# A recommendation tower on one core: six moves issued by the POOL instead of ACT, and two steps of the drain put elsewhere

## What is computed

```python
x = layer_norm(dense_t @ Wd.T, gd, bd)
y = layer_norm(jnp.einsum('bnd,ed->bne', sparse_t, Ws), gs, bs)
y = jnp.einsum('bne,pn->bep', y, Wsi)
y = layer_norm(y, gsi, bsi)
T = jnp.concatenate([x[:, None, :], jnp.swapaxes(y, 1, 2)], axis=1)
Z = jnp.einsum('bnd,bmd->bnm', T, T)
z = layer_norm(Z[:, TRIL_I, TRIL_J] @ Wl.T, gl, bl)      # the first 384 of 512 are kept
h = jnp.concatenate([z, r_dense_t], axis=1)
h = jnp.maximum(h @ W_top1 + b_top1, 0.0)
h = jnp.maximum(h @ W_top2 + b_top2, 0.0)
y = h @ W_top3
```

## Time and profile before

| | us |
|---|---|
| median of 3 timed runs | 590.68 |
| lowest and highest | 590.22, 592.27 |
| the profiled execution | 590.11 |
| its span, first to last instruction | 588.3 |
| PE busy in the span | 523.2 (89%) |
| DVE busy | 431.7 (73%) |
| POOL busy | 394.8 (67%) |
| ACT busy | 339.3 (58%) |

### The profile page before, as it was taken

One profiled execution on the slowest core, in us unless ns is written; L12 is line 12 of the kernel. 1 busy time (PEld: TensorE's weight loads), 2 busy tenths in 40 slices (PEclk: granted clock), 3 DMA queues, 4 the chain that ended last, 5 costly groups with the idle time before them and its releaser, 6 DMA issues.

```text
span 588.3 us, 11685 instructions
## 1 busy us (share of the span) xinstructions
PE 523.2 (89%) x4327; PEld 382.3 (65%) x4327; DVE 431.7 (73%) x806; ACT 339.3 (58%) x731; POOL 394.8 (67%) x420
## 2 busy tenths in 40 slices
PE   0557889597999999997999999998999999989888
PEld 0435656474778667776677767766777767856657
DVE  3579998689677977697877967796787977787210
ACT  1235666466657765575766765675657765766223
POOL 5777777777777777777777777777777777750000
PEclk9997999899899999999999999999999999999999
DMA  6911121212111121212121221212121211110100
GB/s 214 372 47 26 28 54 27 53 28 52 29 42 38 39 62 28 52 30 71 28 46 33 45 56 35 45 31 69 29 52 27 52 31 43 38 34 17 27 0 1
DMA packets 28152, 29.89 MB, mean 51 GB/s; under 512 B 9784, under 2 KB 20544, under 8 KB 27712
## 3 DMA queue, kind: packets, MB, share of 16 engines
q0 software_dynamic: 13312, 13.66, 12.2%
q1 hardware_dynamic: 14456, 15.29, 8.2%
q10 hardware_dynamic: 328, 0.20, 0.1%
HBM read 23.01 MB, written 0.01 MB: 39 GB/s over the span
## 4 chain that ended last, share of the span: by engine, by line
POOL 46%; PE 26%; issue 19%; DMA 4%; DVE 3%; ACT 1%; ACTq 1%; POOLq 0%; SPq 0%
POOL emb L314 46%; PE bank_h L442 5%; PE bank_u L405 4%; DMA emb<-in_tables,ids 3%; PE bank_m L465 3%; PE bank_y L416 3%; PE bank_g L391 2%; PE bank_z L430 2%; PE bank_t L382 2%; PE bank_t L430 1%; PE bank_m L526 1%; DVE part L910 1%; ACTq L774 1%; PE bank_g L490 1%; PE bank_m L533 0%
## 5 line engine op out<-in xcount | busy, mean ns | idle before, releaser
L314 POOL DMA_INDIRECT emb<-in_tables,ids x416 | 394.6, 949 | 130.3 <-issue 123.1
L662 ACT ACTIVATE sq<-tt 128x512 f32<-128x512 f32 x128 | 131.1, 1133 | 4.6 <-DVE tt L963 3.4
L932 DVE TENSOR_TENSOR prod<-bank_g,emb 128x512 f32<-128x512 f32 (+1 forms) x64 | 37.6, 588 | 89.0 <-PE bank_g L391 88.5
L442 PE MATMUL bank_h<-wz,zr 128*128 128x512 f32 x192 | 93.2, 610 | 3.1 <-ACT zt L727 2.1
L405 PE MATMUL bank_u<-mix_w,emb 128*128 128x192 f32 (+4 forms) x512 | 86.0, 314 | 9.7 <-DVE emb L951 9.7
L405 PEld LDWEIGHTS bank_u<-mix_w,emb 128*128 128x128 f32 x512 | 80.3, 200 | 10.9 <-DVE emb L951 10.9
L963 DVE TENSOR_TENSOR tt<-bank_y,biasc 128x512 f32<-128x512 f32 x128 | 81.9, 681 | 2.5 <-PE bank_y L416 2.5
L644 ACT COPY embt<-bank_t 128x512 f32<-128x512 f32 (+1 forms) x64 | 32.5, 507 | 82.4 <-PE bank_t L382 82.2
L980 DVE TENSOR_TENSOR tt<-tt,bank_z 128x1024 f32<-128x1024 f32 x64 | 78.1, 1220 | 2.2
L970 DVE TENSOR_REDUCE ssum<-sq 128x32 f32<-128x1024 f32 x64 | 77.5, 1211 | 1.1 <-ACT sq L662 1.0
L416 PE MATMUL bank_y<-us,proj 64*128 64x512 f32 x256 | 73.0, 647 | 0.7 <-ACT us L654 0.7
(11 more groups left out here) (121 smaller groups left out, 622.5 us busy)
## 6 DMA issues: line engine op xcount, KB each, us to landing
emb<-in_tables,ids POOLq DMA_INDIRECT x416, 2.4
zs<-zbig SPq DMA_DIRECT2D x62, 40.5 KB
zs<-zbig SPq DMA_DIRECT2D x62, 36.0 KB
dense<-in_dense SPq DMA_DIRECT2D x8, 256.0 KB, 5.1
wfull<-in_wfull SPq DMA_DIRECT2D x1, 2048.0 KB, 10.2
wz<-in_wrows SPq DMA_DIRECT2D x1, 1536.0 KB, 13.2
w<-in_w SPq DMA_DIRECT2D x1, 1280.0 KB, 13.9
zs<-zbig SPq DMA_DIRECT2D x62, 16.5 KB
```

The costliest lines, as they stand in the source:

```text
L314: pool.indirect_dma_start(emb[:, e, t, D * a:D * a + D], None, x_in["tables"], bass.IndirectOffsetOnAxis(ap=ids[:, col:col + 1], axis=0),) ...
L442: mm = pe.matmul(bank_h[:, :], zr[:, s, :], wz[:, s, :], start=(s == 0), stop=(s == SLOTS - 1))
L662: A(sq[:, GRP * a:GRP * a + GRP, :].rearrange("p (q w) v -> p q v w", w=WIDE), tt[:, u % 2, q0:q0 + n, C0:ZC, :], ACT.Square).then_inc(sq_ ...
```

## The change

Three things. The six moves of unit 15 that ACT issued (`move_rest`) are gone from ACT; the POOL issues them after its last gather, behind the same three waits, and they count up a semaphore of their own, `zs_rest`, for which `z_rows(15)` waits besides. `gains_z(14)` is due one step sooner, TAIL+5, which puts it behind `relu1(6, 0)` and ahead of `z_rows(15)`. And `open_last` is put from behind `top2(6)` (TAIL+6) to behind `turn_z(15)` and `top3(6)` (TAIL+7), ahead of `last1(0)`.

```diff
 def gains_z_of(s):
     if s > TAIL + 2:
-        return {TAIL + 6: NU - 2, TAIL + 8: NU - 1}.get(s)
+        return {TAIL + 5: NU - 2, TAIL + 8: NU - 1}.get(s)
     return unit(s, GAINZ_AT)
...
+            pool.wait_ge(zc_ok, 4 * NR * NU)
+            pool.wait_ge(sumcol_ok, NU)
+            pool.wait_ge(zr_ok, NU - 1)
+            for j in range(2, 4):
+                for part in range(3):
+                    pool.dma_start(rows_to(j, part), rows_from((NU - 1) % 2, j, part)
+                                  ).then_inc(zs_rest, 16)
...
-                if s == TAIL + 6:
-                    open_last()
                 i = x_of(s, 0)
...
                 j = top3_of(s)
                 if j is not None:
                     top3(j)
+                if s == TAIL + 7:
+                    open_last()
                 a = half_of(s, LAST1_AT)
...
             def z_rows(u):
-                act.wait_ge(zs_in[u % 2], 12 * 16 * (u // 2 + 1))
+                if u < NU - 1:
+                    act.wait_ge(zs_in[u % 2], 12 * 16 * (u // 2 + 1))
+                else:
+                    act.wait_ge(zs_in[u % 2], 12 * 16 * (u // 2) + 6 * 16)
+                    act.wait_ge(zs_rest, 6 * 16)
                 after(act, flat_done, u)
...
-            def move_rest():
-                act.wait_ge(zc_ok, 4 * NR * NU)
-                act.wait_ge(sumcol_ok, NU)
-                act.wait_ge(zr_ok, NU - 1)
-                for j in range(2, 4):
-                    for part in range(3):
-                        act.dma_start(rows_to(j, part), rows_from((NU - 1) % 2, j, part)
-                                      ).then_inc(zs_in[(NU - 1) % 2], 16)
...
-                if pd == (NU - 1, 3):
-                    move_rest()
```

More of the change, by code:

```diff
@@ L268, in dlrm @@
         xcol_ok, z_done, zc_ok, sumcol_ok = sem("xcol_ok"), sem("z_done"), sem("zc_ok"), sem("sumcol_ok")
-        zs_in, zr_ok = [sem("zs_in0"), sem("zs_in1")], sem("zr_ok")
+        zs_in, zs_rest, zr_ok = [sem("zs_in0"), sem("zs_in1")], sem("zs_rest"), sem("zr_ok")
         flat_done, hst_ok, hmv_ok, hstd_ok, hrs_ok, zn_ok = (
```

## The result

The changed kernel took 592.26 us at the median of 22 timed runs (590.27 to 593.93), the kernel before beside it 590.21 (589.73 to 592.59): a ratio of 1.0027, 95% interval 1.0016 to 1.0038. The medians lie 2.05 us apart and the ratio says 0.27%, or 1.6 us: small, but clear of no change, and several times the +0.27 us (0.05%) of the sum. The times of both kernels lie in groups: before, 17 runs from 589.73 to 590.68 and 5 from 592.03 to 592.59; after, 5 from 590.27 to 591.08, 13 from 591.88 to 592.94, and 4 from 593.58 to 593.93. Between the lowest groups there is little, and the changed kernel is seldom in its lowest group. The profiled execution (592.19, span 590.4) is of the middle one.

What follows compares the result with a forecast made beforehand. The prediction took the drain to be bound by a chain of waits between ACT and PE, after a body paced by gathers. Its terms, -1.48 - 0.05 + 1.80 = +0.27 us, on the 590.68 median gave 590.95; range 589.1 to 592.6.

Steps and rivals of the forecast that it cites:

- the sum: In the drain after the body: -1.48 for moves, -0.05 for scaling, +1.80 for open_last, together +0.27 us.
- moves: Six issues leave ACT, so the first rectified pair, relu1(6, 0), starts at 552.76 instead of 554.24: 1.48 us earlier.
- scaling and copy in place of the pair: On ACT before the wide-weights product: scaling and copy take 2.00 us where rectified pair and scaling took 2.05, saving 0.05.
- open_last: Sixteen matmuls moved from PE's idle window before the transposes to its gapless stretch behind the third layer: +1.80 us.
- rival 4: Scaling on ACT not gated, copy comes as the moves land, product starts at 558.62: -1.4 us, 589.3; chance 0.06.
- Rival 1: PE has slack behind the third layer, or open_last held up the transposes, so its cost isn't paid in full: 589.15; chance 0.12.
- The POOL's price: Each of the POOL's six moves costs one gather, 1.25 us start to start; the last lands at 557.74.
- The slack before the copy was due: Moves, due on ACT at about 559.35, have 1.6 us to spare at one gather's price.
- rival 2: POOL issues slowly and delays the product: 0.3% slower at 1.86 us per issue, 595.6 at 2.5; chance 0.18.
- Rival 3: PE's new idle 2.0 us before the transposes brings the lower clock, costing up to 2.5 us: 593.4; chance 0.04.

Runs made afterwards that it cites:

- the own tile: Changed kernel, open_last back behind the second layer, unit 14's scaled rows in a separate tile: 586.76 us, ratio 0.9926; a second version kept ACT's moves, ratio 1.0012.
- open_last back: Changed kernel with open_last returned to behind the second layer (TAIL+6), the POOL's moves and earlier scaling kept: 591.29 us, ratio 0.9985.
- the control: The changed kernel unaltered, measured once more (also called "again") on the chip of three other kernels: 592.64 us, ratio 1.003.
- both gaps filled: Changed kernel with eight calls of matmuls nobody uses, 1.8 us, in each of PE's two idle gaps: 591.06 us, ratio 0.9995.

## Why the prediction was right, and where it wasn't

**The sum.** At the upper level of the clock it is +0.29 to +0.31 us against +0.27, and each term by itself came out: -1.46 for -1.48 (moves), 0.00 for -0.05 (scaling and copy in place of the pair), +1.79 for +1.80 (open_last). What carried it was reading the condition in `gains_z`. By rival 4, the naive reading, the product would have started at 558.6; it started at 560.37, forecast 560.25, and the kernel with the scaling moved alone shows ACT standing 6.4 us in the wait. Rival 1 (slack on PE) fell by the kernel with open_last moved alone.

**The POOL's price** was taken at one gather, 1.25 us; it is 0.57 from issue to issue and 1.9 to landing, where 2.49 was taken. The true value lay below the lower bound, 0.795, which had come from SP. So the bound was none, a rate of one engine saying nothing about another's. It changed nothing, since the moves were hidden at either price. The POOL also began later than forecast, 0.68 us after the start of the last copy of products where ACT had begun 0.42 after it. The slack before the copy was due wasn't 1.6 us. The last of the POOL's moves starts at 552.1 and lands at most 2.1 us later, at 554.2; in the kernel with the own tile, with the same moves, the copy had to wait for data until 555.42, so SP's own half is what lands last, 4 us before the 559.49 at which the copy ran. (In rival 2 the landing that makes the kernel 0.3% slower should be 560.87 for 560.79, which changes nothing.) The Trainium skill ("DMA: Bandwidth & Descriptors", section "Issuing engine by pattern") says that the hardware path of SP and ACT is generally faster; for these moves the rows show 0.57 us per issue on the POOL against 0.795 on SP, and the measurement decides.

**What it had wrong: the clock.** The sum has no term for a fall of the clock behind either gap, and so the forecast for the median, 590.95 within 0.4, missed: the median is 592.26. 590.95 describes the lowest group, and the median is one fall higher. Rival 3 had such a fall, but only behind the new gap before the transposes, at a chance of 0.04. The gap before the product passed for harmless, since it was there before. Yet in all three profiles of a kernel that has it as in the changed one (changed, again, open_last back) the fall came behind that gap. The ground for 0.04 was one row: 2.47 us of idling with the clock at 1.00 behind it. One execution shows one draw. Gaps of one length bring a fall at one time and none at another: the product took 7.11 to 7.12 us in three profiles behind a gap of 2.02 to 2.03, 5.39 in three others behind 2.07 (before, the POOL's moves alone, open_last moved alone), 5.42 behind 2.03 in a fourth (scaling sooner alone, where the clock had fallen in the first layer just before), and 5.42 behind 3.3. A fall costs 1.6 to 1.7 us; rival 3 allowed "up to 2.5". With PE kept busy in the first gap, the product ran at the upper level in all six profiles: four with unused matmuls, two with the own tile.

That the measured median lies inside the range is luck. The upper end, 592.6, was set by rival 2, for a POOL of up to 1.9 us per issue, and the POOL took 0.57; falls of the clock were put outside, at 593.4. What filled the room was a thing for which it hadn't been made. That the kernel before has falls as well, 5 of 22 runs in its upper group, could have been suspected from its three times: 590.22, 590.68 and 592.27. The prediction didn't ask where the 2 us between them come from.

**What stays open.** The kernel before also has two gaps of some 2 us (553.06 to 555.13 and 559.73 to 561.78 in its profile), yet 5 of 22 runs were up against 17 of 22 of the changed kernel; on the chip of the control it was 15 of 29 against 11 of 12. Why the gaps of the changed kernel bring a fall more often isn't settled; that their work before and behind differs is only a guess. With the POOL's moves alone 5 of 12 runs were up, with the scaling sooner besides (open_last back) 8 of 12; that is too few to tell whether the order on ACT matters. The body has falls too: in windows of 5 us, the clock of before is under 0.97 between 40 and 55, 110 and 120, and 145 and 155 us, and that of the changed kernel in about the same places and from 275 to 285. With both gaps filled the body has the same falls as in the changed kernel, and yet all twelve runs lie in one group; so, as far as one profile of each tells, what parts the runs of the changed kernel into groups is the drain. For the kernel before this isn't shown, since no execution of its upper group was profiled.

## What to carry to other kernels

Before a step is moved forward in a queue, read every condition in its body, for the buffer that it overwrites may hold it where it was, and what stands behind it is then held up too; the gain, some 2.3 us, came when the buffer was split. A step that fills a pause should not be moved into a full stretch, however much it looks like order: it costs its whole length there, and leaves a pause in which the clock can fall. Where timed runs lie in groups, look for the row that differs between two profiles, and compare such kernels by a stretch of the profile that is free of what differs elsewhere.

## What the runs showed of the hardware

- Two microseconds without a matmul could be followed, 0.5 to 1.4 us into the work behind them, by some 3 us at the lower clock level, at a cost of 1.6 to 1.7 us, or by no fall at all; eight calls of no use in each of two gaps took 1.58 us off the median. The Trainium skill ("TensorE: Matmul & The Clock Gate", Part 1) says that activity releases the throttle; the filled gaps agree, with a granted clock of 1.00 through the drain of the profile and all twelve runs within 1.1 us.
- A plain move within SBUF of 16.5 to 40.5 KB was issued by the POOL in 0.57 us and landed 1.9 us after its start; SP needs 0.795 per issue. With eighteen in a row the busy time of one rose from 0.58 to 0.70 us.
- At the same clock the twelve matmuls of the product add 5.15 us to the chain directly behind others and 5.39 to 5.42 behind a wait for ACT, be it of 0.24 or of 3.3 us. The ends of matmuls are modelled, but the drain confirms it: with the own tile it is 0.23 to 0.26 us shorter than the gap of 2.07 alone explains.
